# Decoder layer with a mixture of experts: the expert stage in three fp32r passes, the plan and the first weights moved into the stage before

## The reference, cut to what matters

```python
x = layernorm(x + attn(x))                    # 16 heads: block-local windows, and 64 chosen queries over all keys
x = layernorm(x + cross(ctx, ctx, masks, x))  # softmax(scores * x), masked
x = layernorm(x + moe(x))                     # 8 experts of width 352, two of them per token, and a shared one of 704

scores = softmax(x @ gate_w);  topk_w, topk_idx = top_k(scores, 2)
g = silu(x @ w_gate[e]) * (x @ w_up[e])       # for each token's two experts e
routed = sum over its e of topk_w[e] * (g @ w_down[e])
shared = silu(x @ sw_gate) * (x @ sw_up) @ sw_down
```

## Time and profile before

| | |
|---|---|
| median of 3 runs | 1193.27 us (1190.8 to 1193.4) |
| the profiled execution | 1194.69 us, span 1193.0 us |
| busy, PE / DVE / ACT / POOL | 1033.2 / 548.6 / 442.6 / 424.7 us |
| mean granted TensorE clock | 0.933 of full speed |
| first x turned in `experts` to its last product's start | 812.4 to 1151.5 us |

### The profile page before, as it was taken

One profiled execution on the slowest core, in us unless ns is written; L12 is line 12 of the kernel. 1 busy time (PEld: TensorE's weight loads), 2 busy tenths in 40 slices (PEclk: granted clock), 3 DMA queues, 4 the chain that ended last, 5 costly groups with the idle time before them and its releaser, 6 DMA issues. The chain is left out here.

```text
span 1193.0 us, 16414 instructions
## 1 busy us (share of the span) xinstructions
PE 1033.2 (87%) x4682; PEld 653.1 (55%) x4683; DVE 548.6 (46%) x1171; ACT 442.6 (37%) x762; POOL 424.7 (36%) x423
## 2 busy tenths in 40 slices
PE   5999995899999999925999999927899999999960
PEld 4557883444443443314888889914456556555530
DVE  3325435776777777208788888620111111111104
ACT  3332210567667676624444444301112212212114
POOL 2000000255465464445566666312223233233224
PEclk9999997799999999956999999967989999999985
DMA  7454306234244242042111111107973333343327
GB/s 244 154 186 159 141 1 129 55 82 106 68 90 105 55 104 54 1 132 84 54 54 54 54 53 53 45 10 255 269 198 61 63 70 57 66 69 55 70 36 282
DMA packets 80876, 115.66 MB, mean 97 GB/s; under 512 B 15680, under 2 KB 37056, under 8 KB 80832
## 3 DMA queue, kind: packets, MB, share of 16 engines
q1 hardware_dynamic: 65648, 90.17, 26.0%
q0 software_dynamic: 9760, 20.49, 9.5%
q10 hardware_dynamic: 5424, 4.46, 1.2%
HBM read 74.77 MB, written 40.31 MB: 96 GB/s over the span
## 5 line engine op out<-in xcount | busy, mean ns | idle before, releaser
L553 POOL TENSOR_TENSOR pair_sum<-probs 128x2048 f32<-128x2048 f32 x32 | 146.1, 4565 | 164.1 <-ACT probs L692 164.1
L717 DVE TENSOR_REDUCE maxima<-ps_s 128x8 f32<-128x512 f32 x256 | 168.6, 689 | 71.4 <-PE ps_s L585 69.6
L692 ACT ACTIVATE probs<-ps_st 128x512 f32<-128x512 f32 x256 | 146.6, 600 | 93.1 <-PE ps_st L634 89.6
L1532 POOL DMA_INDIRECT x_dram<-e_y,who x39 | 62.1, 1593 | 215.0 <-ACT e_y L1557 211.1
L585 PE MATMUL ps_s<-k,q 96*128 96x512 f32 x256 | 115.4, 458 | 14.7 <-DMA k<-qk_dram 11.8
L634 PE MATMUL ps_st<-q,k 128*128 128x512 f32 x256 | 121.2, 475 | 4.8 <-ACT probs L692 2.5
L1583 DVE COPY e_gT<-e_ps_gT 128x384 f32<-128x384 f32 x39 | 21.7, 557 | 215.0 <-PE e_ps_gT L1622 215.0
L634 PEld LDWEIGHTS ps_st<-q,k 128*128 128x128 f32 x256 | 49.2, 193 | 109.7 <-ACT probs L692 77.0
L1614 PE MATMUL e_ps_g<-w_all,xgT 128*128 x312 | 106.7, 487 | 2.7 <-DMA w_all<-in_L_ffn_w_down_dram 2.0
L1630 PE MATMUL e_ps_y<-w_all,e_gT 128*128 (+1 forms) x234 | 107.0, 593 | 0.8 <-DVE e_gT L1583 0.8
L1614 PE MATMUL e_ps_u<-w_all,xgT 128*128 x312 | 99.0, 460 | 0.0
(11 more groups left out here) (224 smaller groups left out, 1851.3 us busy)
## 6 DMA issues: line engine op xcount, KB each, us to landing
qk_dram<-qk_ctx SPq DMA_DIRECT2D x32, 512.0 KB, 2.8
q<-qk_dram SPq DMA_DIRECT2D x96, 128.0 KB
k<-qk_dram SPq DMA_DIRECT2D x96, 128.0 KB
w_all<-in_L_ffn_w_gate_dram SPq DMA_DIRECT2D x8, 704.0 KB
w_all<-in_L_ffn_w_up_dram SPq DMA_DIRECT2D x8, 704.0 KB
x_dram<-x SPq DMA_DIRECT2D x16, 256.0 KB, 2.1
x_dram<-attn SPq DMA_DIRECT2D x16, 256.0 KB
w_all<-in_L_ffn_w_down_dram SPq DMA_DIRECT2D x8, 512.0 KB
```

What stands on the lines that cost most here:

```text
L553: pool.tensor_tensor(pair_sum[:, h], probs[:, 2 * h], probs[:, 2 * h + 1], ALU.add).then_inc(added, 1)
L692: act.activation(probs[:, kc, j, :], ps_st[:, s % 2, :], ACT.Exp, scale=SCALE).then_inc(exp_done, 1)
L717: dve.tensor_reduce(by_tile[:, t, j, 1:9], ps_s[:, x % 2, :].rearrange("p (g n) -> p g n", n=S // 8), axis=AX.X, op=ALU.max).then_inc(s_re ...
L1532: pool.indirect_dma_start(out=x3_dram[:], out_offset=bass.IndirectOffsetOnAxis(ap=who[:, j, 0:1], axis=0), in_=y[:, p, :], in_offset=None, ...
```

## The change

- `plan` is no block of its own any more. Its DVE chain runs at the end of DVE's stream in `cross_and_shared`, its sum over partitions at the end of PE's, its two iotas in POOL's ahead of the last `send`. Its tiles lie in `x_in` and a PSUM tile of that stage.
- SP loads expert 0's weights in `cross_and_shared`, after all tiles but before the last store of x3. `w_all` now lies over `qk_ctx`, `attn` and what follows them, so it waits until the last scores are done. The load of experts 1 to 7 stays where it was.
- In `experts`, each product is three fp32r passes as in the cross stage. For every tile ACT copies the expert's gate, up and down weights (1408, 1408 and 1536 columns) into `w_hi`, and DVE subtracts into `w_lo`; both engines read the expert's number into a register before it. There is one buffer of each. x and g are split in the same way.
- `xg` has four buffers, `list_in` waits for the list two before and no longer for its gather, and the scatter comes four tiles after the gather instead of three. A tile's down product takes all 128 rows of its third chunk; POOL fills the 32 rows that no weight stands in with zeros, once. x out of PSUM and the down product have two PSUM buffers. Four tiles make one turn of the loop.

```diff
+def load_expert(sp, c, e, w_gate, w_up, w_down, w_in):
...
@@ cross_and_shared, SP
                 tiles(sp, one)
+                sp.wait_ge(s["sc_done"], NT)
+                sp.wait_ge(s["q_tile_done"], NT)
+                load_expert(sp, c, 0, w_gate, w_up, w_down, c.w_in)
                 store_x3(NT - 1, B - 1, TT - 1)
@@ cross_and_shared, POOL
                 tiles(pool, one)
+                pool.iota(plan_tiles.at_i, pattern=[[P, NT]], base=0, channel_multiplier=0)
+                pool.iota(plan_tiles.tile_i, pattern=[[1, NJ]], base=0, channel_multiplier=0).then_inc(s["plan_built"], 1)
                 send(NT - 1, (NT - 1) % 2)
@@ cross_and_shared, DVE
                 locate(NT - 1)
+                plan(dve, c, plan_tiles, s)
@@ cross_and_shared, PE
                 ranks(NT - 1)
+                pe.wait_ge(s["slots_done"], NT)
+                pe.matmul(plan_tiles.ps_count, ones[:], both_sum[:], start=True, stop=True).then_inc(s["plan_counted"], 1)
@@ experts
+        def expert_base(eng, j):
+            e = eng.value_load(c.expert_of[0:1, bass.ds(j, 1)], min_val=0, max_val=E - 1)
+            eng.wait_ge(c.w_in, 64 * e + 64)
+            return e * WCOLS
@@ experts, SP
-                    need(sp, s[f"x_in{p}"], 16 * ((j - p) // 2) if isinstance(j, int) else 8 * (j - p))
+                    need(sp, s[f"who{p}"], 16 * ((j - p) // 2) if isinstance(j, int) else 8 * (j - p))
...
                 for e in range(E):
                     if e:
-                        sp.wait_ge(s["w_in"], 64 * e)
-                    weights_in(e)
+                        sp.wait_ge(c.w_in, 64 * e)
+                        load_expert(sp, c, e, w_gate, w_up, w_down, c.w_in)
                     list_in(e + 2, e % 2)
@@ experts, POOL (gather: xg[:, j % XG, :], need(pool, s["turned"], j - XG + 1))
+                for j in range(NJ + XG):
+                    if j < NJ:
+                        gather(j)
+                    if j == 1:
+                        pool.wait_ge(s["padded"], 1)
+                        pool.memset(w[FCR:P, :]...[:, :, WCOLS - D:WCOLS], 0.0).then_inc(s["zeroed"], 1)
+                    if j >= XG:
+                        scatter(j - XG, j % 2)
@@ experts, ACT
+                def w_high(base, kind):
+                    act.activation(w_hi[kind][:], raw(base, kind), ACT.Copy).then_inc(s[kinds[kind] + "_hi"], 1)
+                def down_high(j):
+                    base = expert_base(act, j)
+                    need(act, s["y_done"], j)
+                    w_high(base, DOWN)
+                def hidden_high(j):
+                    base = expert_base(act, j)
+                    need(act, s["g_done"], j)
+                    w_high(base, GATE)
+                    need(act, s["u_done"], j)
+                    w_high(base, UP)
+                def one(j, r):        # guards for the first and last tiles left out
+                    down_high(j - 1)
+                    x_high(j + 1, 1 - p)
                     silu(j, p)
+                    g_high(j - 1, 1 - p)
+                    y_store(j - 2, p)
+                    hidden_high(j + 1)
@@ experts, DVE
+                def w_low(j, kind):
+                    base = expert_base(dve, j)
+                    dve.wait_ge(s[kinds[kind] + "_hi"], j + 1)
+                    dve.tensor_tensor(w_lo[kind][:], raw(base, kind), w_hi[kind][:].bitcast(F32),
+                                      ALU.subtract).then_inc(s[kinds[kind] + "_lo"], 1)
+                def one(j, r):        # guards left out
+                    w_low(j, UP)
+                    w_low(j - 1, DOWN)
+                    g_low(j - 1, 1 - p)
+                    x_low(j + 1, 1 - p)
                     multiply(j, p)
+                    w_low(j + 1, GATE)
@@ experts, PE
+                def passes(out, stationary, moving, chunks):
+                    for q in range(chunks):
+                        for k, (a, z) in enumerate(((0, 0), (0, 1), (1, 0))):
+                            last = pe.matmul(out, stationary[a](q), moving[z](q), start=(q == 0 and k == 0),
+                                             stop=(q == chunks - 1 and k == 2))
+                    return last
+                def one(j, r):        # guards left out
+                    x_turn(j + 1, (r + 1) % XG)
+                    hidden(j, p, GATE)
+                    g_turn(j - 1, 1 - p)
+                    hidden(j, p, UP)
+                    down(j - 1, 1 - p)
```

More of the change, by code:

```diff
@@ L1 @@
+import math
 from contextlib import ExitStack
@@ L774, in _, with plan_memory, take, plan @@
                 units(dve, unit)
+def plan_memory(m, x_in, ps_xT):
+    t = Kept()
+    free = x_in[:].rearrange("p a d -> p (a d)")
+    at = 0
+    def take(*dims):
+        nonlocal at
+        n = math.prod(dims)
+        view, at = free[:, at:at + n], at + n
+        return view.rearrange("p (a b) -> p a b", b=dims[-1]) if len(dims) > 1 else view
+    t.past, t.gone, t.more = take(NJ, E), take(NJ, E), take(E, NT)
+    t.count, t.length, t.end = take(E), take(E), take(E)
+    t.e_of, t.start, t.row, t.tile, t.at = take(NJ), take(NJ), take(NJ), take(NJ), take(NT)
+    t.at_i, t.tile_i = m.sb("at_i", [P, NT], I32)[:], m.sb("tile_i", [P, NJ], I32)[:]
+    t.ps_count = ps_xT[:, 0:E]
+    return t
+def plan(dve, c, t, s):
+    k = 0
+    def link(ins):
+        nonlocal k
+        k += 1
+        ins.then_inc(s["plan_step"], 1)
+        dve.wait_ge(s["plan_step"], k)
+    dve.wait_ge(s["plan_built"], 1)
+    dve.tensor_copy(t.at, t.at_i)
+    link(dve.tensor_copy(t.tile, t.tile_i))
+    dve.wait_ge(s["plan_counted"], 1)
+    link(dve.tensor_copy(t.count, t.ps_count))
+    link(dve.tensor_tensor(t.more, t.count.rearrange("p (e a) -> p e a", a=1).to_broadcast([P, E, NT]),
+                           t.at.rearrange("p (a n) -> p a n", a=1).to_broadcast([P, E, NT]), ALU.is_gt))
+    link(dve.tensor_reduce(t.length, t.more, axis=AX.X, op=ALU.add))
+    link(dve.tensor_copy(t.end, t.length))
+    for e in range(1, E):
+        link(dve.tensor_tensor(t.end[:, e:e + 1], t.end[:, e:e + 1], t.end[:, e - 1:e], ALU.add))
+    link(dve.tensor_tensor(t.past, t.tile.rearrange("p (j a) -> p j a", a=1).to_broadcast([P, NJ, E]),
+                           t.end.rearrange("p (a e) -> p a e", a=1).to_broadcast([P, NJ, E]), ALU.is_ge))
+    dve.tensor_tensor(t.gone, t.past, t.length.rearrange("p (a e) -> p a e", a=1).to_broadcast([P, NJ, E]), ALU.mult)
+    link(dve.tensor_reduce(t.e_of, t.past, axis=AX.X, op=ALU.add))
+    link(dve.tensor_reduce(t.start, t.gone, axis=AX.X, op=ALU.add))
+    link(dve.tensor_tensor(t.row, t.tile, t.start, ALU.subtract))
+    link(dve.tensor_scalar(t.row, t.row, float(P), None, ALU.mult))
+    link(dve.scalar_tensor_tensor(t.row, t.e_of, float(T), t.row, ALU.mult, ALU.add))
+    dve.tensor_copy(c.first_row[:], t.row[0:1, :])
+    dve.tensor_scalar(c.expert_of[:], t.e_of[0:1, :], float(E - 1), None, ALU.min)
 EPS = 1e-5
@@ L1473, in experts, with tiles @@
         s = {k: m.sem("e_" + k) for k in names}
         top = E * T + (NJ - 1) * P
-        def pairs(eng, one, first, last):
-            assert first % 2 == 1 and (last - first) % 2 == 1
-            one(first, 1)
-            one(first + 1, 0)
-            with eng.Fori(1, (last - first + 1) // 2) as i:
-                one(2 * i + first, 1)
-                one(2 * i + first + 1, 0)
+        kinds = ("gate", "up", "down")
+        def tiles(eng, one):
+            for j in range(3):
+                one(j, j)
+            with eng.Fori(0, (NJ - 7) // XG) as i:
+                for k in range(XG):
+                    one(XG * i + 3 + k, (3 + k) % XG)
+            for j in range(NJ - 4, NJ):
+                one(j, j % XG)
@@ new lines, in at, with is_last, arrived, raw @@
+        def at(j, low):
+            return not isinstance(j, int) or j >= low
+        def is_last(j):
+            return isinstance(j, int) and j == NJ - 1
+        def arrived(j, r):
+            return 16 * ((j - r) // XG) + 16 if isinstance(j, int) else (16 // XG) * (j - r) + 16
+        def expert_base(eng, j):
+            e = eng.value_load(c.expert_of[0:1, bass.ds(j, 1)], min_val=0, max_val=E - 1)
+            eng.wait_ge(c.w_in, 64 * e + 64)
+            return e * WCOLS
+        def raw(base, kind):
+            cols = piece_cols(kind)
+            return w[:, bass.ds(base + cols.start, cols.stop - cols.start)]
@@ new lines, in hidden @@
+                def hidden(j, p, kind):
+                    out = ps_u if kind == UP else ps_g
+                    if kind == GATE:
+                        pe.wait_ge(s["xT_lo_done"], j + 1)
+                        need(pe, s["silu_done"], j)
+                    else:
+                        need(pe, s["g_ready"], j)
+                    pe.wait_ge(s[kinds[kind] + "_lo"], j + 1)
+                    passes(out[:, 0:FH], [lambda q, t=t: t[:, p, q * P:(q + 1) * P] for t in (xT_hi, xT_lo)],
```

(2 more changed lines are left out.)

246 lines of the change are left out of this document (93 added, 153 removed).

## The result

The changed kernel takes 1149.56 us (median of 4 runs, 1148.1 to 1150.03); the kernel before took 1192.03 us in the same series. The ratio is 0.9643 with a 95% interval of 0.9627 to 0.966, so about 42.5 us less. The profiled execution took 1150.03 us, span 1148.3.

What follows compares the result with a forecast made beforehand. Past its first 72 us the expert stage was bound by TensorE's own work. Savings 17.5 + 30 x (8.17 - 7.1) - 0.4 - 0.6 = 48.6 us gave 1145 us, 8 in 10 within 1131 to 1176.

Steps and rivals of the forecast that it cites:

- TensorE's work: Expert stage: three fp32r passes at the cross stage's pace take 6.73 us a tile instead of 8.11.
- VectorE's and ScalarE's work: Expert stage: splitting weights, x and g for each tile takes VectorE 6.74 us and ScalarE 6.44 us.
- Register loads: Expert stage, before ScalarE's and VectorE's weight operations: loading the expert's number hides behind earlier work, 0 to 0.2 us.
- 0.52 for the third: VectorE in a tile: the instruction ahead of the third register load lasts only 0.52 us, the other two 1.6.
- bare registers: Rival, VectorE in the experts: three uncovered loads of 0.75 us make a tile 8.99 us, total 1202 us; chance 0.11.
- The period: Steady stretch of the experts: tiles 7.1 us apart instead of 8.17, ends 6.8 and 7.6.
- the 6.81 loop: Expert tile: gate matmuls, g transposes, g high, store of y, gate copy, gate subtract and hand-overs, 6.81 us, longest found.
- Port: Rival, experts: VectorE's two-SBUF-input subtractions and POOL's DMA issues exclude each other, period 7.9, total 1169 us; chance 0.13.
- a sign of the port: Expert stage: subtractions longer than 1.61 us or POOL's issues above 1.6 us would show the shared port.
- Joint: Between cross and expert stages: the plan block's 6.7 us go, its work hidden behind the last scatter at cost 0.
- Head: First expert tiles: steady stretch starts 17.5 us earlier (14 to 20), from plan, expert 0's load, buffers and lists.
- End: End of the expert stage: last tile's exposed work costs 0.4 us more, clearing ten more semaphores 0.6.

Runs made afterwards that it cites:

- the last experiment: Changed kernel with lists ahead, loads spread, VectorE's register earlier, last down copy earlier; then y's store behind ScalarE's copies, its register ahead of g high: 1168.29 us.
- The joint alone: The kernel before with only plan and expert 0's load moved into the cross stage's tail, experts otherwise old: 1182.7 us, ratio 0.9938.

## Why the prediction was right

**TensorE's work.** Forecast 6.73 us a tile; without register work the period is 6.77, TensorE busy 180.00 of 180.00 us there. Right.

**VectorE's and ScalarE's work.** Each term within 1% (1622 ns against 1.61 us, 1752 against 1.76, 1374 against 1.36). Right, and it means that prices read from a stage of the same kernel with the same shape carry over. Their sums are a little high: instructions that wait for nothing start some 0.08 us before the one ahead has ended, and busy time is 6.5 us a tile for VectorE and 6.0 for ScalarE (179.83 and 166.56 of 200 us), not 6.74 and 6.44. So ScalarE is at 83% and VectorE just short of 90%, where the forecast wanted all three engines above 90%.

**Register loads.** Here a term failed. Forecast: 0 to 0.2 us a tile. Measured: 0.46. The prediction itself named the case, "0.52 for the third", and then took the value of the covered ones. The step that failed is that 0.52 us of cover was priced like 1.6. The gap of 0.49 stands behind the 0.52 us of the product, so the register work takes about 1.0 us from the time the product has started, somewhat more than SP's 0.75; VectorE's two loads behind 1.6 us cost nothing. That settles the rival too: bare registers at 3 x 0.75 a tile would need all three exposed, and one was, in part, with perhaps a tenth of a microsecond of ScalarE's. The Trainium skill, "TensorE: Matmul & The Clock Gate", the table at its head, gives VectorE a queue of 8; by that the load should run ahead of the work. The trace agrees for two loads of three: each was hidden up to the length of the one instruction in front of it. The product in front of the third waits for TensorE itself, so this load had no earlier work to run behind; whether more than one instruction could hide a load no run here shows.

**The period, 7.1 forecast and 7.22 measured.** The value was nearly right for another reason than given. The 0.3 us put on top of the 6.81 loop for small waits is nearly the price of the register (6.77 + 0.46 = 7.23). Nor is it the forecast's loop that sets the pace, since the gate copy in it is done early. It is one that the forecast did not list: gate product, g transposes, up product, VectorE's product, gate subtraction. With the forecast's own terms it is 1.93 + 0.33 + 1.93 + 0.2 + 0.52 + 1.61 + 0.2 = 6.72 us, and with the 0.49 of the register 7.21. The forecast's loop comes first only once that register is out of the way, at 6.9 us. So the number is in part luck: a missing loop and a register priced at nothing were covered by an allowance for something else. The 30 tiles gave 28.4 us instead of 32.1, and these 3.7 are the largest miss of the sum.

**Port.** Forecast a rival of 0.13, 1169 us. The subtractions are not lengthened (1622 ns) and the period doesn't move without the scatters. But the two do meet: a gather's issue within the subtractions takes 2.14 us on the mean, above the 1.6 that the forecast had named as a sign of the port, where one in the kernel before took 0.98. In the last experiment it is the scatter that pays (2.72 against 1.59) while the gather, now issued mostly outside them, is back at 1.09. Within the changed kernel, too, a gather issued beside x low and the product, which read PSUM, takes the short time (timeline):

```profile
851.38 0.98 POOL L1560 DMA_INDIRECT xg<-x_dram,who  x1 [6.53 <-DMA x_dram<-e_y,who]
```

ScalarE's copies are not the cause: the scatter at 944.85 lies wholly within two of them and takes 1.59. The size varies: in the run without register loads and in the one without scatters a gather takes 1.7 us. POOL pays, VectorE does not, and POOL had the room until its issue moved onto the path of the rows. The Trainium skill, "SBUF — State Buffer", section "Who interferes with whom", states that the two contend, and infers that descriptor writing is spared. The traces bear the first half out, on POOL's side. For the issue of an indirect DMA as a whole they are against the inference; whether it is the reading of the list of rows or the writing of descriptors that is held, no run tells.

**Joint.** 6.9 us saved against 6.7, the plan wholly behind the last scatter. Right.

**Head.** 18.0 us (19.4 less the cross stage's 1.4) against 17.5. The sum was right, its parts were not. Forecast: 6.7 for the joint, 10.3 for the load, 1 for buffers and lists, and "three passes save nothing" where TensorE waits. The joint alone shows 7.0 + 4.2 by its trace, so 6.8 of the 18.0 need the rest of the change. Of these the four buffers hold 2 to 4 us and the lists' waits 0 to 2; what is left, 1 to 5 us, is the faster tiles, by subtraction only. TensorE waits in the head for gathers, but between the waits it works, and the gather of a later tile waits for its turn: a faster tile lets the chain go on earlier. And with the old waits of the lists expert 1's load is held 3.5 us by a list that waits for a gather, which I had not followed along SP's queue.

**End.** Forecast -1.0, measured -3.1. The added 0.4 us for the last tile was too small: with nothing else to work on, TensorE sees store, down copy, down subtraction and g low one behind the other (4.79 us of wait), and then works at half its clock, 9 x 0.2 = 1.8 us more. The wait before counted on work that has none behind it in the last tile.

**Sum.** 17.5 + 32.1 - 1.0 = 48.6 forecast; 18.0 + 28.4 - 3.1 = 43.3 measured, and 1.4 from the cross stage's end make 44.7.

## What to carry to other kernels

A register load on a compute engine was covered here by the one instruction ahead of it: put it behind the longest of the loop. When several engines end within a few tenths of each other, write down every loop through them, also the one through each engine's short work, and list every queue that an instruction feeds before moving it; moving a store by 2.7 us cost 36 us through a scatter and the gather behind it. And an edit that starts a chain of loads earlier is worth what the work behind the chain can take up: the same early load gave at most 4 us to the kernel with slow tiles and 10 to the one with fast ones.

## What the runs showed of the hardware

- The register work of a weight operation on VectorE took about 1.0 us from the start of the instruction ahead of it: a 0.52 us one left 0.49 bare, a 1.6 us one nothing. On ScalarE 0.2 to 0.33 us were bare behind silu's 0.47 in most tiles, up to 1.0 in a few.
- An indirect DMA's issue on POOL within VectorE's subtractions with two SBUF inputs took 0.7 to 1.2 us longer (gather 0.98 to 2.14, and to 1.7 in two of the experiments; scatter 1.59 to 2.72). The subtractions were not slower.
- After 5 us in which TensorE worked 0.5, nine matmuls of 512 columns came at a granted clock of 0.50 (1.2 GHz), 0.43 us apart instead of 0.233. In the run without scatters the clock fell within the nine, behind the same wait (4.78 us): 0.62 on the mean.
